# Mamba stack: half the square of the clipped exponential formed on ScalarE, softplus in four VectorE instructions per half, silu of z in the window that uses it

## The chip, the cores and the metric

The kernel runs on one core of a Trainium2 chip. The metric is the device time in microseconds (us) of one execution; the median of three runs of the kernel before is 5499.93 us (5496.72 to 5500.54).

## The reference

Four Mamba layers run over a batch of four sequences (64 conditioning tokens in front of 512 tokens, width 256, inner width 512, 16 states), and three transformer layers follow, which the change does not touch. One Mamba block, cut to what matters:

```python
xz = einsum('bsd,ed->bse', rmsnorm(h, norm_w), ip_w)
xi, z = split(xz, 2, axis=-1)
xi = silu(causal_conv(xi, cw) + cb)
dt, Bm, Cm = split(einsum('bse,fe->bsf', xi, xp_w), [DR_, DR_ + DS_], axis=-1)
dt = softplus(einsum('bsr,er->bse', dt, dtp_w) + dtp_b)
dA = exp(dt[..., None] * -exp(A_log))
dBu = dt[..., None] * Bm[:, :, None, :] * xi[..., None]
# scan over time: h = dA * h + dBu;  y = sum over states of h * C
y = (y + xi * Dp) * silu(z)
h = h + einsum('bse,de->bsd', y, op_w)
```

Softplus of v is taken as relu(v) + log(1 + e) with e = exp(-|v|). The kernel uses the logarithm of (1 + e) / (1 + EDGE) for large e and the series m - m*m/2 with m = min(e, EDGE), EDGE = 2^-11, for what is below.

## The kernel before, in words

The Mamba stack is 16 units of work, one per layer and batch entry, and the code walks them in "windows": window n does the scan of unit n, the preparation of unit n+1 and the end of unit n-1 together. Window -1 only prepares unit 0; it is the prologue. Channels lie on the 128 partitions; a unit has 4 chunks of 128 channels by T = 576 tokens, and a "half" is two chunks, 1152 columns. A window has 32 steps j: 16 states for either half.

In step j each engine has a fixed share of the scan, written out by hand:

- ScalarE (ACT), `decay(j)`, line 515: two exponentials of 128x575 make DA for step j. It is issued two steps ahead, and may be at most four steps ahead of the scan, since DA has four buffers. Decays 0 and 1 of a window wait for the semaphore s_dt, with which VectorE says that the step sizes DT of that unit are complete.
- VectorE (DVE), `drive(j)`, line 630, multiplies DTX by the row of B into PSUM (U); `recur(j)`, line 638, is the scan of 128x1152. The scan waits for its DA (semaphore s_da).
- GpSimd (POOL), line 571, multiplies the states by C; TensorE (PE), line 356, adds them up into Y.

Between these steps the preparation of the next unit is placed by tables. `PREP_AT` gives the steps of the TensorE products and of the ScalarE reads behind them: the mean square "ms" in step 0, the projections "xz" (0 to 3 for x, 4 to 7 for z), the convolution "cv", "xp", and "dt" in steps 24 to 27. In step 0 ScalarE also squares the stream for the norm (line 437), TensorE sums the squares (ms), and ScalarE takes the logarithm and exponential of the sum (lines 442 and 444); `norm()` on VectorE (line 598) uses that after step 3.

`prep_read("dt", i)` on ScalarE writes relu(v) to DT and |v| to E (a view of XPAD), and after every second chunk the exponential E (line 471) and the logarithm LG (line 472), and raises s_sp. `softplus(k, part_two)` on VectorE, lines 606 to 622, then finishes a half. `SOFTPLUS` places part one of the first half behind step 27, part two behind 28, and those of the second half behind 30 and 31. Part two of the second half raises s_dt.

`silu_z` on ScalarE, lines 504 to 507, loads the table with silu, applies it to all 2304 columns of z of unit n+1, and loads the table of exp and ln again. `SILU_Z` places it in step 30. `gate` on VectorE (line 645) multiplies Y by silu(z): the first half of a unit behind step 17 of its own window, the second half behind step 2 of the next one.

Of the kernel before, what the change touches and what calls it, by code (L numbers as in the profile page):

```python
# [6 lines left out]
ALU = mybir.AluOpType  # L7
# [3 lines left out]
P = 128  # L11
D = 256
KD = D // P
# [3 lines left out]
START = 1  # L17
# [13 lines left out]
PAD = DC - 1  # L31
EDGE = 2.0 ** -11
SHRINK = 1.0 / (1.0 + EDGE)
NBC = 2 * DS
NXP = NBC + DR

# [36 lines left out]
           16: ("xz", 4), 18: ("cv", 2), 20: ("cv", 3), 22: ("xp", 0), 23: ("xz", 5), 24: ("dt", 0), 25: ("dt", 1),  # L73
           26: ("dt", 2), 27: ("dt", 3), 28: ("xz", 6), 29: ("xz", 7)}
END_AT = {6: ("O", 0), 8: ("O", 1)}
SILU_X, SILU_Z = 21, 30

SOFTPLUS = {27: (0, False), 28: (0, True), 30: (KD, False), 31: (KD, True)}
NBB = 4
# [22 lines left out]
def mamba_stack(nc, hT, IDENT, wa, wb, x_t, ctx_t, pre_w, ones, fin_norm):  # L102
# [3 lines left out]
    with ctx:  # L106
# [15 lines left out]
        FIN = sb("FIN", [P, KD])  # L122
        EPSC = sb("EPSC", [P, 1])
        SHRC = sb("SHRC", [P, 1])
        HN = sb("HN", [P, KD, T])
        RSTD = sb("RSTD", [P, T])
        XPAD = sb("XPAD", [P, KI, PAD + T])
# [79 lines left out]
        with nc.Block() as block:  # L207
# [191 lines left out]
            def _(act):  # L399
# [12 lines left out]
                def body(n, scan, prep, end):  # L412
# [3 lines left out]
                    npar = nxt % 2  # L416
                    off = npar * (KI * T)
                    hb = (nxt % NB) * T
                    k0 = 8
                    step = [0]  # L420

                    def own(ins, wait=True):
# [16 lines left out]
                    def prep_read(kind, i):  # L439
                        full(kind, i)  # L440
                        if kind == "ms":
                            own(act.activation(half(RSTD[:, :]), pair, ACT.Ln, bias=EPSC[:, 0:1]))
                            act.sem_inc(s_free, 1)
                            act.activation(RSTD[:, :], RSTD[:, :], ACT.Exp, scale=-0.5).then_inc(s_rstd, 1)
                        if kind == "xz" and i < KI:
                            act.activation(half(XPAD[:, i, PAD:PAD + T]), pair, ACT.Copy).then_inc(s_xi, 1)
                            act.wait_ge(s_xi, START + nxt * KI + i + 1)
                            act.sem_inc(s_free, 1)
                        if kind == "xz" and i >= KI:
                            act.activation(half(ZS[:, bass.ds(off + (i - KI) * T, T)]), pair, ACT.Copy).then_inc(s_z, 1)  # L450
                            act.wait_ge(s_z, START + nxt * KI + i - KI + 1)
                            act.sem_inc(s_free, 1)
                        if kind == "cv":
                            act.activation(half(XS[:, bass.ds(off + i * T, T)]), pair, ACT.Identity,
                                           bias=WA[:, A_CB + i:A_CB + i + 1]).then_inc(s_conv, 1)
                            act.wait_ge(s_conv, START + nxt * KI + i + 1)
                            act.sem_inc(s_free, 1)  # L457
                        if kind == "xp":
                            if scan:
                                act.wait_ge(s_rows, 16 * nxt)  # L460
                            act.activation(half(BCF[:, :]), PAIR[0:NXP, :, 0:HT], ACT.Copy).then_inc(s_bcf, 1)
                            act.wait_ge(s_bcf, START + nxt + 1)
                            act.sem_inc(s_free, 1)
                        if kind == "dt":
                            bias = WA[:, A_DTB + i:A_DTB + i + 1]
                            act.activation(half(DT[:, bass.ds(off + i * T, T)]), pair, ACT.Relu, bias=bias)
                            own(act.activation(E[:, i, :].rearrange("p (a n) -> p a n", a=2), pair, ACT.Abs, bias=bias))
                            act.sem_inc(s_free, 1)
                            if i % 2:
                                two = slice(i - 1, i + 1)  # L470
                                own(act.activation(E[:, two, :], E[:, two, :], ACT.Exp, scale=-1.0))
                                act.activation(LG[:, two, :], E[:, two, :], ACT.Ln, bias=SHRC[:, 0:1],
                                               scale=SHRINK).then_inc(s_sp, 1)
                            if i == KI - 1:
                                own(act.activation(ALOG[:, :], WA[:, A_LOG:A_COLS], ACT.Exp))
                                act.activation(NEGA[:, bass.ds(npar * (KI * DS), KI * DS)], ALOG[:, :], ACT.Copy,
                                               scale=-1.0).then_inc(s_nega, 1)
# [25 lines left out]

                    def silu_z():
                        act.preload_act_table_set("silu_and_others")
                        act.activation(ZS[:, bass.ds(off, KI * T)], ZS[:, bass.ds(off, KI * T)], ACT.Silu).then_inc(s_zs, 1)
                        act.preload_act_table_set("natural_log_exp_and_others")

                    def decay(j):
# [15 lines left out]
                    for j in range(NJ):  # L525
                        if prep and j == 0:
                            squares()
                        if prep and j == SILU_X:
                            silu_x()
                        if prep and j == SILU_Z:  # L530
                            silu_z()
                        if scan and j + 2 < NJ:
                            decay(j + 2)
                        if prep and j in (2, 3) and nxt % NB == 0:
                            diagonals(j - 2)
                        for kind, i in slot_uses(j, prep, end):
                            if kind == "O":
                                stream(i)
                            else:
                                prep_read(kind, i)  # L540
                    assert not prep or step[0] == k0, step
                act.wait_ge(s_zero, START + 3)
                act.wait_ge(s_dvec, 16 * NL)
                act.wait_ge(s_const, 32)
                windows(body)
# [12 lines left out]
            def _(pool):  # L558
                pool.memset(EPSC[:, :], EPS).then_inc(s_zero, 1)
                pool.memset(SHRC[:, :], SHRINK).then_inc(s_zero, 1)  # L560
                pool.memset(DA[:, :, :], 0.0).then_inc(s_zero, 1)

                def body(n, scan, prep, end):
# [12 lines left out]
            def _(dve):  # L576
                def body(n, scan, prep, end):
# [4 lines left out]
                    hb = (nxt % NB) * T  # L582
                    eoff = par * (KI * T)
                    uses, base = window_uses(prep, end), before(n, N_PREP, N_END)
                    k_prep = 10
                    start = before(n, k_prep, 0)
                    step = [0]

# [17 lines left out]
                    def softplus(k, part_two):  # L606
# [2 lines left out]
                        o = off + k * T  # L609
                        dt = DT[:, bass.ds(o, KD * T)].rearrange("p (c t) -> p c t", c=KD)  # L610

                        e, ln, part = E[:, k:k + KD, :], LG[:, k:k + KD, :], E[:, k:k + KD, :]
                        if not part_two:
                            own(dve.tensor_scalar(part, e, EDGE, -0.5, ALU.min, ALU.mult))
                            own(dve.scalar_tensor_tensor(out=part, in0=part, scalar=1.0, in1=part, op0=ALU.add, op1=ALU.mult))
                        else:
                            own(dve.scalar_tensor_tensor(out=dt, in0=part, scalar=-2.0, in1=dt, op0=ALU.mult, op1=ALU.add))
                            own(dve.scalar_tensor_tensor(out=dt, in0=ln, scalar=0.0, in1=dt, op0=ALU.max, op1=ALU.add))
                            own(dve.tensor_tensor(DTX[:, bass.ds(o, KD * T)], DT[:, bass.ds(o, KD * T)],
                                                  XS[:, bass.ds(o, KD * T)], ALU.mult))  # L620
                            if k:
# [1148 lines left out]
```

## Time and profile before

| | |
|---|---|
| median of three runs | 5499.93 us |
| the profiled execution's own time | 5501.36 us |
| its span, first to last instruction | 5499.6 us |
| PE busy | 4949.9 us (90%) |
| DVE busy | 3920.6 us (71%) |
| POOL busy | 2606.0 us (47%) |
| ACT busy | 2303.9 us (42%) |
| Mamba stack, of the span | 0 to about 2465 us |

Busy shares are means over two very different parts. In the Mamba part (the first 18 of the 40 slices of the page) VectorE is busy nearly all of the time; in the transformer part TensorE is. Idle time in front of an instruction is printed in square brackets in the timeline, with the engine or queue that ended it.

### The profile page before, as it was taken

To read this page: it belongs to the slowest core of one execution; us is meant where nothing else is said; L and a number is where in the kernel's file an instruction comes from. 1 tells how busy PE (TensorE), PEld (TensorE's weight loads), DVE (VectorE), ACT (ScalarE), POOL (GpSimd) and SP (SyncE) were. 2 spreads that over 40 slices of the span, in tenths; PEclk is the share of its full clock that TensorE was granted. 3 is DMA by queue.
4 is the path that set the end of the run, shared out by engine and by line. 5 is a ranking of instruction groups with operands and counts; after the bars stand their busy time and mean duration, and the time that the engine had idled before them with its cause. 6 is when DMAs were issued, how large, how long until landed. Compare 5 with 4: busy or idle time off the path is not lost.

```text
span 5499.6 us, 53836 instructions
## 1 busy us (share of the span) xinstructions
PE 4949.9 (90%) x18976; PEld 2623.3 (48%) x18976; DVE 3920.6 (71%) x3886; ACT 2303.9 (42%) x4022; POOL 2606.0 (47%) x1334
## 2 busy tenths in 40 slices
PE   5888898888888888877999889999999999999999
PEld 3455555555555555433444444444444444444444
DVE  2999999999999999974767552666656246665641
ACT  3555654455555555523444333333333233333321
POOL 1555555555555555554777212666610036665000
PEclk8999999999999999987999999999999999999999
DMA  2434444444444444321000010000000000001000
GB/s 78 142 132 148 145 147 147 142 144 144 144 144 140 140 144 144 134 107 36 1 1 21 19 39 1 1 1 1 10 38 31 8 1 1 1 1 47 0 1 16
DMA packets 94440, 376.70 MB, mean 68 GB/s; under 512 B 13024, under 2 KB 14432, under 8 KB 91232
## 3 DMA queue, kind: packets, MB, share of 16 engines
q1 hardware_dynamic: 94176, 373.26, 19.4%
q8 instruction: 157, 2.57, 0.2%
q14 instruction: 107, 0.88, 0.1%
HBM read 369.94 MB, written 3.28 MB: 68 GB/s over the span
## 4 chain that ended last, share of the span: by engine, by line
PE 43%; DVE 6%; POOL 3%; issue 1%; ACT 1%; DMA 0%; SPq 0%; DVEq 0%; ACTq 0%
PE PS L1061 6%; PE PS L1085 6%; PE PS L1071 5%; PE PS L1246 5%; PE PS L1040 5%; PE PS L1257 3%; POOL PA L1004 3%; PE PS L1049 3%; PE PS L1095 3%; PE PS L1206 2%; PE PS L1170 1%; PE PS L1158 1%; DVE PA L1582 1%; DVE CST L1580 1%; DVE NMX L1494 1%
## 5 line engine op out<-in xcount | busy, mean ns | idle before, releaser
L571 POOL TENSOR_TENSOR UH<-UH,BC 128x1152 f32<-128x1152 f32 x512 | 1343.7, 2624 | 1094.2 <-DVE U L630 1094.2
L1004 POOL TENSOR_SCALAR PA<-PA,INV 128x512 f32<-128x512 f32 x768 | 1188.1, 1563 | 647.8 <-DVE INV L1500 645.4
L356 PE MATMUL Y<-UH,ident_sb 128*128 128x512 f32 (+1 forms) x3072 | 1171.1, 526 | 226.4 <-POOL UH L571 171.8
L638 DVE TENSOR_TENSOR_SCAN UH<-DA,U 128x1152 f32<-128x1152 f32 x512 | 1307.2, 2553 | 21.2 <-ACT DA L515 3.8
L356 PEld LDWEIGHTS Y<-UH,ident_sb 128*128 128x128 f32 x3072 | 591.3, 203 | 844.9 <-issue 569.9
L1317 ACT ACTIVATE PA<-PS,NMX 128x512 f32<-128x512 f32 x768 | 521.0, 683 | 1028.9 <-DVE NMX L1494 1002.8
L515 ACT ACTIVATE DA<-DT,NEGA 128x575 f32<-128x575 f32 x1024 | 718.8, 763 | 333.5 <-DVEq L622 237.5
L630 DVE TENSOR_TENSOR U<-DTX,BC 128x1152 f32<-128x1152 f32 x512 | 701.1, 1369 | 49.5 <-DVEq L622 4.2
L1494 DVE TENSOR_REDUCE NMX<-PS 128x2 f32<-128x1024 f32 x384 | 467.8, 1219 | 242.6 <-PE PS L1061 242.3
L1509 DVE COPY VP<-PS 128x512 f32<-128x512 f32 x768 | 491.9, 681 | 32.2 <-PE PS L1071 31.7
L1071 PEld LDWEIGHTS PS<-ident_sb,PA 128*128 128x128 f32 x3072 | 330.1, 142 | 327.4 <-issue 195.3
L1071 PE MATMUL PS<-ident_sb,PA 128*128 128x128 f32 x3072 | 437.3, 282 | 21.5 <-POOL PA L1004 20.6
L1061 PE MATMUL PS<-QK 64*128 64x512 f32 (+1 forms) x1536 | 435.9, 645 | 4.7 <-issue 2.5
L1085 PE MATMUL PS<-VP 128*64 128x256 f32 (+1 forms) x3072 | 375.0, 386 | 0.1
L992 POOL TENSOR_TENSOR LSQ<-stream 128x512 f32<-128x512 f32 x21 | 26.6, 1266 | 694.8 <-DVE stream L1599 437.7
L1040 PE MATMUL PS<-HN,W 128*128 128x512 f32 x640 | 309.8, 606 | 5.1 <-DVEq L1489 2.9
L312 PE MATMUL PAIR<-HN,WA 128*128 128x288 f32 x1024 | 278.3, 416 | 14.6 <-DVE HN L598 6.4
L1246 PE MATMUL PS<-HN,VP 128*128 128x512 f32 x640 | 288.6, 592 | 2.7 <-issue 2.7
L1486 DVE TENSOR_SCALAR QK<-PS,VEC 128x512 f32<-128x512 f32 x80 | 64.8, 810 | 303.7 <-PE PS L1040 303.7
L1085 PEld LDWEIGHTS PS<-VP 128*64 128x64 f32 (+1 forms) x3072 | 191.3, 128 | 168.7 <-issue 46.2
L312 PE MATMUL PAIR<-XPAD,DG 128*128 128x288 f32 x1024 | 259.8, 406 | 3.3 <-ACTq L457 1.8
L1634 DVE SCALAR_TENSOR_TENSOR QK<-PS,VEC,QK 128x512 f32<-128x512 f32 x64 | 48.1, 751 | 244.5 <-ACT QK L1413 244.5
(133 smaller groups left out, 5443.1 us busy)
## 6 DMA issues: line engine op xcount, KB each, us to landing
BC<-bc_rows SPq DMA_DIRECT2D x512, 576.0 KB, 3.7
WA<-mamba_a SPq DMA_DIRECT2D x16, 1421.0 KB, 7.4
W<-pair_w SPq DMA_DIRECT2D x6, 3072.0 KB, 10.4
WB<-mamba_b SPq DMA_DIRECT2D x16, 514.0 KB, 5.0
VP<-ff_w SPq DMA_DIRECT2D x2, 3072.0 KB
WO<-out_w SPq DMA_DIRECT2D x4, 1024.0 KB
stream<-x_t SPq DMA_DIRECT2D x2, 1024.0 KB, 6.9
VP<-ff_w SPq DMA_DIRECT2D x2, 1024.0 KB
```

Source lines behind the costliest of these rows:

```text
L312: mm = pe.matmul(PAIR[0:out_rows, a, 0:HT], lhs, rhs(a), start=start, stop=stop)
L356: mm = pe.matmul(Y[:, a:b], IDENT[:, :], UH[:, SLOT[j], a:b], start=(s == 0), stop=(s == DS - 1), skip_group_check=True)
L515: ins = act.activation(DA[:, j % NDA, c * T + 1:(c + 1) * T], DT[:, bass.ds(par * (KI * T) + cc * T + 1, T - 1)], ACT.Exp, scale=NEGA[:, b ...
L571: pool.tensor_tensor(h, h, BC[:, j % NBB, 1, :].unsqueeze(1).broadcast_to([P, HK, T]), ALU.mult).then_inc(s_hc, 1)
L630: dve.tensor_tensor(u, x, BC[:, j % NBB, 0, :].unsqueeze(1).broadcast_to([P, HK, T]), ALU.mult).then_inc(s_u, 1)
L638: dve.tensor_tensor_scan(UH[:, SLOT[j], :], DA[:, j % NDA, :], U[:, 0:HC], 0.0, ALU.mult, ALU.add).then_inc(s_scan, 1)
L1004: pool.tensor_scalar(PR[:, n % 3, j, :], PR[:, n % 3, j, :], INV[:, n % 4, j:j + 1], None, ALU.mult).then_inc(s_ps, 1)
L1040: mm = pe.matmul(PS[:, B_J, :], w_tile(l, "qk".index(kind), t, k), HN[:, k, b * S0:(b + 1) * S0], start=(k == 0), stop=(k == KD - 1))
L1061: mm = pe.matmul(PS[:, B_S + 2 * (n % 2) + j, :], Q[r:r + HW[l], tt % 2, qt * P:(qt + 1) * P], K[r:r + HW[l], tt % 2, :], start=True, stop ...
L1071: mm = pe.transpose(PS[:, B_T + j, kt * P:(kt + 1) * P], PR[:, n % 3, j, kt * P:(kt + 1) * P], IDENT[:, :])
L1085: mm = pe.matmul(PS[r:r + HW[l], B_V, half * 256:(half + 1) * 256], VT[:, tt // QT % 2, kt, c:c + HW[l]], PT[:, hh % 2, kt, j, :], start=( ...
L1246: mm = pe.matmul(PS[:, 2 * (f % 2) + g, :], w1[:, k, c:c + P], HN[:, k, b * S0:(b + 1) * S0], start=(k == 0), stop=(k == KD - 1))
```

## The change

The silu of z goes from step 30 of the window that prepares the unit to step 1 of the window that scans it. ScalarE forms half the square of m, by a relu and a square of 128x1152 per half, and puts it into DTX, which is free until the product with x is written there. VectorE then adds the logarithm and m to DT in part one, and subtracts the half square and multiplies by x in part two: four instructions per half where there were five. Two memsets of GpSimd in the prologue fill the constants EDGC.

```diff
-SILU_X, SILU_Z = 21, 30
+SILU_X, SILU_Z = 21, 1
...
                             if i % 2:
                                 two = slice(i - 1, i + 1)
                                 own(act.activation(E[:, two, :], E[:, two, :], ACT.Exp, scale=-1.0))
-                                act.activation(LG[:, two, :], E[:, two, :], ACT.Ln, bias=SHRC[:, 0:1],
-                                               scale=SHRINK).then_inc(s_sp, 1)
+                                act.activation(LG[:, two, :], E[:, two, :], ACT.Ln, bias=SHRC[:, 0:1], scale=SHRINK)
+                                sq = DTX[:, bass.ds(off + (i - 1) * T, KD * T)].rearrange("p (c t) -> p c t", c=KD)
+                                own(act.activation(sq, E[:, two, :], ACT.Relu, bias=EDGC[:, 0:1], scale=-1.0))
+                                act.activation(sq, sq, ACT.Square, bias=EDGC[:, 1:2], scale=-HALF_ROOT).then_inc(s_sp, 1)
...
                     def silu_z():
                         act.preload_act_table_set("silu_and_others")
-                        act.activation(ZS[:, bass.ds(off, KI * T)], ZS[:, bass.ds(off, KI * T)], ACT.Silu).then_inc(s_zs, 1)
+                        act.activation(ZS[:, bass.ds(par * (KI * T), KI * T)], ZS[:, bass.ds(par * (KI * T), KI * T)],
+                                       ACT.Silu).then_inc(s_zs, 1)
                         act.preload_act_table_set("natural_log_exp_and_others")
...
-                        if prep and j == SILU_Z:
+                        if scan and j == SILU_Z:
                             silu_z()
...
-                        e, ln, part = E[:, k:k + KD, :], LG[:, k:k + KD, :], E[:, k:k + KD, :]
+                        e, ln = E[:, k:k + KD, :], LG[:, k:k + KD, :]
                         if not part_two:
-                            own(dve.tensor_scalar(part, e, EDGE, -0.5, ALU.min, ALU.mult))
-                            own(dve.scalar_tensor_tensor(out=part, in0=part, scalar=1.0, in1=part, op0=ALU.add, op1=ALU.mult))
+                            own(dve.scalar_tensor_tensor(out=dt, in0=ln, scalar=0.0, in1=dt, op0=ALU.max, op1=ALU.add))
+                            own(dve.scalar_tensor_tensor(out=dt, in0=e, scalar=EDGE, in1=dt, op0=ALU.min, op1=ALU.add))
                         else:
-                            own(dve.scalar_tensor_tensor(out=dt, in0=part, scalar=-2.0, in1=dt, op0=ALU.mult, op1=ALU.add))
-                            own(dve.scalar_tensor_tensor(out=dt, in0=ln, scalar=0.0, in1=dt, op0=ALU.max, op1=ALU.add))
+                            own(dve.tensor_tensor(DT[:, bass.ds(o, KD * T)], DT[:, bass.ds(o, KD * T)],
+                                                  DTX[:, bass.ds(o, KD * T)], ALU.subtract))
                             own(dve.tensor_tensor(DTX[:, bass.ds(o, KD * T)], DT[:, bass.ds(o, KD * T)],
                                                   XS[:, bass.ds(o, KD * T)], ALU.mult))
```

The first place is ScalarE at the turn from window 0 to window 1 (every later turn is alike). The rows of before begin at the last read of z. DA rows are decays, two to a step; the four together are those of steps 0 and 1, the next two are step 2, the last ones step 3 and on.

```order
L450 ACTIVATE ZS<-PAIR 128x576
L505 ACT_TABLE_LOAD
L506 ACTIVATE ZS<-ZS 128x2304
L507 ACT_TABLE_LOAD
L515 ACTIVATE DA<-DT,NEGA 128x575 x4
L437 ACTIVATE HN<-stream 128x1152
L515 ACTIVATE DA<-DT,NEGA 128x575 x2
L442 ACTIVATE RSTD<-PAIR,EPSC 128x576
L444 ACTIVATE RSTD<-RSTD 128x576
```

The same place in the changed kernel, whose line numbers are a few higher:

```order
L452 ACTIVATE ZS<-PAIR 128x576
L520 ACTIVATE DA<-DT,NEGA 128x575 x4
L439 ACTIVATE HN<-stream 128x1152
L520 ACTIVATE DA<-DT,NEGA 128x575 x2
L444 ACTIVATE RSTD<-PAIR,EPSC 128x576
L446 ACTIVATE RSTD<-RSTD 128x576
L509 ACT_TABLE_LOAD
L510 ACTIVATE ZS<-ZS 128x2304
L512 ACT_TABLE_LOAD
```

The block of two table loads and the silu stood ahead of the decays of step 0; now it stands behind the norm's exponential and ahead of the decays of step 3.

The second place is VectorE behind steps 27 and 28 of a window. L638 is the scan, L630 the drive of the next step. Before:

```order
L638 SCALAR_TENSOR_TENSOR UH<-DA,U 128x1152
L614 TENSOR_SCALAR XPAD<-XPAD 128x2x576
L615 SCALAR_TENSOR_TENSOR XPAD<-XPAD 128x2x576
L630 TENSOR_TENSOR U<-DTX,BC 128x1152
L638 SCALAR_TENSOR_TENSOR UH<-DA,U 128x1152
L617 SCALAR_TENSOR_TENSOR DT<-XPAD,DT 128x1152
L618 SCALAR_TENSOR_TENSOR DT<-LG,DT 128x1152
L619 TENSOR_TENSOR DTX<-DT,XS 128x1152
L630 TENSOR_TENSOR U<-DTX,BC 128x1152
```

And now, with L645 as the scan and L637 as the drive:

```order
L645 SCALAR_TENSOR_TENSOR UH<-DA,U 128x1152
L621 SCALAR_TENSOR_TENSOR DT<-LG,DT 128x1152
L622 SCALAR_TENSOR_TENSOR DT<-XPAD,DT 128x1152
L637 TENSOR_TENSOR U<-DTX,BC 128x1152
L645 SCALAR_TENSOR_TENSOR UH<-DA,U 128x1152
L624 TENSOR_TENSOR DT<-DT,DTX 128x1152
L626 TENSOR_TENSOR DTX<-DT,XS 128x1152
L637 TENSOR_TENSOR U<-DTX,BC 128x1152
```

Behind the first scan a tensor_scalar is replaced by a scalar_tensor_tensor; behind the second one of three instructions is gone, and the first of the two left is a tensor_tensor.

The third place is ScalarE at the fourth read of dt, in step 27. Before:

```order
L467 ACTIVATE XPAD<-PAIR,WA 128x576
L471 ACTIVATE XPAD<-XPAD 128x2x576
L472 ACTIVATE LG<-XPAD,SHRC 128x1152
L475 ACTIVATE ALOG<-WA 128x64
L476 ACTIVATE NEGA<-ALOG 128x64
L515 ACTIVATE DA<-DT,NEGA 128x575 x2
```

And now:

```order
L469 ACTIVATE XPAD<-PAIR,WA 128x576
L473 ACTIVATE XPAD<-XPAD 128x2x576
L474 ACTIVATE LG<-XPAD,SHRC 128x1152
L476 ACTIVATE DTX<-XPAD,EDGC 128x1152
L477 ACTIVATE DTX<-DTX,EDGC 128x1152
L479 ACTIVATE ALOG<-WA 128x64
L480 ACTIVATE NEGA<-ALOG 128x64
L520 ACTIVATE DA<-DT,NEGA 128x575 x2
```

Two instructions of 128x1152 stand between the logarithm and what followed it; the same two stand behind the logarithm of the first half.

## Rows read from the trace of the kernel before

**Rows 1.** Page, part 2: VectorE's busy tenths in 40 slices

```profile
DVE  2999999999999999974767552666656246665641
```

**Rows 2.** Stages: stretch, length, busy us of each engine, clock, DMA

```profile
111.00:2312.00 2201.00, 1907.77 (x6194) 1134.67 (x6194) 2127.61 (x1185) 1174.21 (x1591) 1257.45 (x479) 0.93 0.41 143
```

**Rows 3.** VectorE's groups by line and shape, 0 to 2300 us

```profile
L638 DVE TENSOR_TENSOR_SCAN UH<-DA,U 128x1152 f32<-128x1152 f32 x479 | 1222.9, 2553 | 20.0 <-ACT DA L515 3.8
L630 DVE TENSOR_TENSOR U<-DTX,BC 128x1152 f32<-128x1152 f32 x479 | 656.0, 1370 | 46.2 <-DVEq L622 4.0 <-DVE UH L638 1.9
L617 DVE SCALAR_TENSOR_TENSOR DT<-XPAD,DT 128x1152 f32<-128x1152 f32 x31 | 45.5, 1468 | 0.1
L615 DVE SCALAR_TENSOR_TENSOR XPAD<-XPAD 128x1152 f32<-128x1152 f32 x31 | 42.1, 1359 | 1.1
L614 DVE TENSOR_SCALAR XPAD<-XPAD 128x1152 f32<-128x1152 f32 x31 | 27.0, 871 | 60.4 <-ACT LG L472 60.4
```

**Rows 4.** VectorE's timeline behind steps 27 and 28 of window 3

```profile
671.27 0.88 DVE L614 TENSOR_SCALAR XPAD<-XPAD 128x1152 f32<-128x1152 f32 x1
...
673.57 1.37 DVE L630 TENSOR_TENSOR U<-DTX,BC 128x1152 f32<-128x1152 f32 x1
...
677.44 1.49 DVE L617 SCALAR_TENSOR_TENSOR DT<-XPAD,DT 128x1152 f32<-128x1152 f32 x1
...
681.75 1.37 DVE L630 TENSOR_TENSOR U<-DTX,BC 128x1152 f32<-128x1152 f32 x1
```

**Rows 5.** ScalarE's timeline at the turn from window 3 to 4

```profile
674.59 1.42 ACT L515 ACTIVATE DA<-DT,NEGA 128x575 f32<-128x575 f32 x2
...
680.55 1.28 ACT L505 ACT_TABLE_LOAD   x1
...
683.98 1.28 ACT L507 ACT_TABLE_LOAD   x1
700.20 2.77 ACT L515 ACTIVATE DA<-DT,NEGA 128x575 f32<-128x575 f32 x4 [14.93 <-DVEq L622]
702.87 1.15 ACT L437 ACTIVATE HN<-stream 128x1152 f32<-128x1152 f32 x1
...
709.46 2.75 ACT L515 ACTIVATE DA<-DT,NEGA 128x575 f32<-128x575 f32 x4
```

**Rows 6.** VectorE's scans: step 30 of window 3, steps 0 and 3 of window 4

```profile
687.21 2.55 DVE L638 TENSOR_TENSOR_SCAN UH<-DA,U 128x1152 f32<-128x1152 f32 x1
...
701.75 2.55 DVE L638 TENSOR_TENSOR_SCAN UH<-DA,U 128x1152 f32<-128x1152 f32 x1
...
714.98 2.55 DVE L638 TENSOR_TENSOR_SCAN UH<-DA,U 128x1152 f32<-128x1152 f32 x1
```

**Rows 7.** TensorE's sum of squares in window 4, from its timeline

```profile
704.16 3.81 PE L312 MATMUL PAIR<-HN,ONES 128*128 128x288 f32 x8 [4.80 <-ACT HN L437]
```

**Rows 8.** ScalarE's decays of steps 0 and 3, windows 3 and 14

```profile
553.81 2.77 ACT L515 ACTIVATE DA<-DT,NEGA 128x575 f32<-128x575 f32 x4 [16.10 <-DVEq L622]
...
562.88 2.76 ACT L515 ACTIVATE DA<-DT,NEGA 128x575 f32<-128x575 f32 x4
...
2165.92 2.77 ACT L515 ACTIVATE DA<-DT,NEGA 128x575 f32<-128x575 f32 x4 [16.22 <-DVEq L622]
...
2175.55 2.75 ACT L515 ACTIVATE DA<-DT,NEGA 128x575 f32<-128x575 f32 x4
```

**Rows 9.** Prologue and window 0, timelines of ScalarE and VectorE

```profile
104.79 0.76 DVE L614 TENSOR_SCALAR XPAD<-XPAD 128x1152 f32<-128x1152 f32 x1 [1.36 <-ACT LG L472]
116.47 2.55 DVE L638 TENSOR_TENSOR_SCAN UH<-DA,U 128x1152 f32<-128x1152 f32 x1 [3.76 <-ACT DA L515]
...
128.64 2.55 DVE L638 TENSOR_TENSOR_SCAN UH<-DA,U 128x1152 f32<-128x1152 f32 x1
...
103.43 1.26 ACT L472 ACTIVATE LG<-XPAD,SHRC 128x1152 f32<-128x1152 f32 x1
...
114.93 2.77 ACT L515 ACTIVATE DA<-DT,NEGA 128x575 f32<-128x575 f32 x4
...
124.56 2.09 ACT L515 ACTIVATE DA<-DT,NEGA 128x575 f32<-128x575 f32 x3
```

More of the change, by code:

```diff
@@ L33 @@
 SHRINK = 1.0 / (1.0 + EDGE)
+HALF_ROOT = 0.5 ** 0.5
 NBC = 2 * DS
@@ L124, in mamba_stack @@
         SHRC = sb("SHRC", [P, 1])
+        EDGC = sb("EDGC", [P, 2])
         HN = sb("HN", [P, KD, T])
@@ L418, in body @@
                     hb = (nxt % NB) * T
-                    k0 = 8
+                    k0 = 10
                     step = [0]
@@ L541, in body @@
                     assert not prep or step[0] == k0, step
-                act.wait_ge(s_zero, START + 3)
+                act.wait_ge(s_zero, START + 5)
                 act.wait_ge(s_dvec, 16 * NL)
@@ L560, in _ @@
                 pool.memset(SHRC[:, :], SHRINK).then_inc(s_zero, 1)
+                pool.memset(EDGC[:, 0:1], EDGE).then_inc(s_zero, 1)
+                pool.memset(EDGC[:, 1:2], EDGE * HALF_ROOT).then_inc(s_zero, 1)
                 pool.memset(DA[:, :, :], 0.0).then_inc(s_zero, 1)
@@ L584, in body @@
                     uses, base = window_uses(prep, end), before(n, N_PREP, N_END)
-                    k_prep = 10
+                    k_prep = 8
                     start = before(n, k_prep, 0)
```

## Prediction

> **What bounds the kernel now.** I read the page's slices first. VectorE stands at 9 tenths in slices 2 to 17, the Mamba part [rows 1]. Over windows 0 to 14 the stage table gives VectorE 2127.61 of 2201.00 us, or 97%, and ScalarE 1174.21, or 53% [rows 2]. The groups by line then say what VectorE's idle time is: ahead of 479 drives 46.2 us and ahead of 479 scans 20.0 us, about 0.1 us each, the handover from one to the next; the only wait for a decay is 3.8 us in all [rows 3], and it lies in the prologue [rows 9]. So no other engine holds VectorE up once the scans run. An instruction taken from it there shortens the kernel by its own length, and each wait that it gets lengthens it. What comes behind the Mamba part starts when that part ends and is not touched.
>
> ScalarE looks free, but its free time is not spread evenly. At each turn between windows it waits for s_dt, 14.93 us here, 16.10 and 16.22 at two others [rows 5, 8]. The silu block sits in front of that wait and costs nothing there. Behind the wait, ScalarE has no lead at all: it has made no DA yet, and four steps' worth must be ready by step 3. That is where the block goes.
>
> **Term 1: VectorE's instructions in softplus.** Before, part one takes 673.57 - 671.27 = 2.30 us from its first start to the drive, and part two 681.75 - 677.44 = 4.31 us [rows 4]. Together 6.61 us per half. Of the new four instructions, three kinds are known: a scalar_tensor_tensor of this size takes 1.36 us when it follows with a wait (line 615) [rows 3], and 1.47 us when it starts right behind a scan (line 617) [rows 3]; the step from one to the next is 0.03 us more. Part one becomes 1.50 + 1.39 = 2.89 us. Part two becomes a tensor_tensor behind a scan and another one. The drive, also a tensor_tensor of 128x1152, takes 1.37 us (line 630) [rows 3], so 1.39 for the second. For the first, whose output is in SBUF and which starts behind a scan, I have no row. Its bounds are 1.36, as alone, and 1.49, as the longest here of the kind behind a scan (line 617) [rows 4]; I take 1.47, since it too has two inputs and follows a scan without a wait. Part two is then 1.50 + 1.39 = 2.89 us. New sum 5.78 us, a gain of 0.83 us per half, with bounds of 0.81 and 0.94. Windows 0 to 14 hold 30 halves: **-24.9 us**, between -24.3 and -28.2.
>
> The gain is small because the removed group is the cheap one: a tensor_scalar of 0.87 us (line 614) [rows 3]. The removed scalar_tensor_tensor is made up for by the new subtraction.
>
> **Term 2: the silu block behind the norm.** In window 4 ScalarE gets s_dt at 700.20. It makes the decays of 0 and 1, the squares, the decay of 2; then it waits for TensorE's sum of squares, which starts at 704.16, right after the squares, and takes 3.81 us [rows 5, 7]. The decay of step 3 starts at 709.46, 9.26 us after s_dt. Now the block comes in between. It lasts from 680.55 to 683.98 + 1.28 = 685.26, 4.71 us [rows 5]. From the start of a decay pair to the scan that waits for it are 116.47 - 114.93 = 1.54 us, by the one place where a scan waits for one [rows 9]. So the scan of step 3 can start at 9.26 + 4.71 + 1.54 = 15.51 us after s_dt. It starts at 714.98 - 700.20 = 14.78 us now [rows 5, 6], and everything ahead of it on VectorE (three steps and the gate of the second half) stays. That makes a wait of 0.73 us in this window; generally it is (distance from s_dt to the decay of 3) - 8.53. The distance is 9.07 in window 3, the shortest, and 9.63 in window 14 [rows 8]; over the 14 windows 1 to 14 its mean is 9.50, as most are at 9.63. Mean wait 0.97, times 14: **+13.6 us**, with 7.6 if all were like window 3 and 15.4 if all were like window 14.
>
> Window 0 has no gate, so its scan 3 comes earlier, at 128.64. The decay of 3 would start at 124.56 + 4.71, its scan at 130.81: **+2.2 us** [rows 9]. Window 15 has no norm to wait for: its decay of 3 stands behind three decays and the block, some 4.1 + 4.7 = 8.8 us after s_dt, and costs nothing.
>
> Queued behind the block are only decays. From step 3 on ScalarE needs 1.4 us per step, VectorE 1.37 + 2.55 and more, so the lead is back by step 5 or 6. The diagonals of windows 3, 7 and 11 (20 copies in steps 2 and 3, some 5.8 us) come after the decays of 4 and 5 and still leave step 6 its DA.
>
> **Term 3: two ScalarE operations per half.** The nearest rows are the square of 128x1152 at 1.15 us (line 437) [rows 5] and the logarithm at 1.26 (line 472) [rows 9]; I take 1.2 each. In the windows they delay the decays of 29 to 31 and the reads of z by 2.4 and then 4.8 us. Decay 30 starts at 674.59; at 679.4 it would still be ready at 680.9, with its scan at 687.21 [rows 5, 6]. 6 us of slack are left. TensorE's last dt and z products wait for those reads and delay the sums of steps 25 to 27, but a scan needs a sum only four steps later. The s_dt wait loses no time, as the 14.93 us stay: the block's 4.7 us leave it, the added 4.8 enter. Cost: nothing. If that cover were gone, it would be up to 4.8 us per window.
>
> The prologue has no cover. The second s_sp, 104.79 now, comes 4 x 1.2 us later, at 109.6, since dt is read one chunk after the other; four instructions of 1.39 bring s_dt to 115.1, the first decay to 115.2 and the first scan to 116.8, against 116.47 [rows 9]. There the block had stood between, and its going saves what the new operations add: **+0.3 us**.
>
> **Sum.** -24.9 + 13.6 + 2.2 + 0.3 = -8.8 us. Against the profiled execution's own 5501.36 that is 5492.6. That execution lies 1.4 us above the median of the runs, so 5491 us on the scale of the median.
>
> **A rule weighed.** The rows show the block as 4.71 us, of which the two loads are 1.28 each and nothing is left between [rows 5]. The Trainium skill (ScalarE: Activation LUTs, section "What ACT_TABLE_LOAD costs") gives the same 1.28 us but adds a drain of about 1.38 for every switch, 2.66 in all. By that rule the block behind the decays would take about 7.4 us, an estimate, and the sum would come out near +32. The trace speaks against it.
>
> **Rivals.**
>
> - *The wait is shorter (14%).* The sum of squares takes 3.81 us at a clock that has dropped while TensorE was idle; window 3 has the shortest distance. If the shorter gap at the turn keeps the higher clock, all windows are like window 3 or better: -24.9 + 7.6 + 1.6 + 0.3 = -15.4, 5484.5. Against it: TensorE is still idle 4 us there.
> - *No wait at all (6%).* ScalarE's place proves free, as its 53% busy suggests: -24.9 + 0.3 = -24.6, 5475. Against it are the times of rows 5 and 6.
> - *Slower: the block holds ScalarE longer when it stands behind exponentials (4%).* Before, it always stood behind a copy or an identity. If each of its two loads first waited for the exponential in front to drain, for as long again as a load lasts (1.28 us), the block would be 7.3 us, and scan 3 would wait 2.6 us more in 15 windows, +39: +30 us, 5530. It decides from a block of 5.3 us on, where no gain is left, and shows as slower from 6.0. The rule weighed above lies on this side.
> - *Slower: ScalarE late at the end of the windows (3%).* If the two operations cost over 3 us each, or TensorE's sums came late, scan 30 would wait. Its slack is 6 us; from there each us of lateness is 15 us, so 1.5 us beyond it end at +14, 5514.
> - *The two terms cancel (7%).* The tensor_tensor or the scalar_tensor_tensor behind the scan costs 0.2 us more than I took: -3, 5497.
>
> **How the numbers follow.** 0.2%, or 11 us, is about what a measurement of this kernel can tell from no change. The forecast itself has 66%, with 5485 to 5495 by its bounds (-28.2 + 13 + 2.5 at one end, -24.3 + 15.4 + 2.5 + 1 at the other). It crosses the 11 us for some 14 of these 66. Faster: 14 + 14 + 6 = 34%. Slower: 4 + 3 = 7%. Same: 52 + 7 = 59%. The range leaves out "no wait at all", the slower rivals and their like: 5479 to 5500.
>
> **What would show it.** VectorE's idle time ahead of the scans, put down to DA, should rise from 3.8 us to some 16 to 18, in 15 pieces, one per window at step 3: 0.5 to 1.2 us each and 2.2 in window 0. The 3.76 us in the prologue should be gone. The first instructions of parts one and two should read 1.47 us, the second ones 1.36. ScalarE's wait for s_dt should remain near 15 us. Most dangerous to the number is the distance from s_dt to the decay of step 3, since every 0.1 us of it is 1.5 us of the result.

## The result, and the profile after

The changed kernel takes 5485.98 us (median of 20 runs, 5471.53 to 5492.46), the kernel before 5496.33 us (median of 20, 5481.84 to 5504.88). The ratio is 0.9984 with a 95% interval of [0.9977, 0.9991]: between 5 and 13 us less, 8.8 by the ratio and 10.4 by the two medians. 5485.98 is inside the stated range of 5479 to 5500, 5 us below the 5491 of the forecast, and the change is within the 0.2% which was the likeliest case. Of those 5 us, 3.6 come from the starting point: the forecast took 5499.93 for the kernel before, from three runs. The profiled execution has a span of 5483.3 us against 5499.6.

The runs of one kernel lie up to 23 us apart, so much of what follows is read from the timelines of single executions, by two numbers: when the first scan starts, and the time from the first to the last scan of the Mamba part, called the stack. There is one profile of each kernel. What lies behind the last scan, untouched by any kernel here, took 3052.5 to 3058.0 us in the eleven profiles. The first scan starts at 117.28 (before 116.47), the last one at 2430.49 (before 2441.61): 2313.21 us between them against 2325.14.

The groups of VectorE, 0 to 2300 us; columns as in [rows 3]:

```profile
L645 DVE TENSOR_TENSOR_SCAN UH<-DA,U 128x1152 f32<-128x1152 f32 x480 | 1225.5, 2553 | 30.2 <-issue 6.3 <-DVE U L637 5.3 <-ACT DA L520 2.3
...
L624 DVE TENSOR_TENSOR DT<-DT,DTX 128x1152 f32<-128x1152 f32 x32 | 47.0, 1468 | 0.1
L621 DVE SCALAR_TENSOR_TENSOR DT<-LG,DT 128x1152 f32<-128x1152 f32 x32 | 46.8, 1463 | 67.0 <-ACT DTX L477 67.0
L622 DVE SCALAR_TENSOR_TENSOR DT<-XPAD,DT 128x1152 f32<-128x1152 f32 x32 | 43.5, 1358 | 1.1
L626 DVE TENSOR_TENSOR DTX<-DT,XS 128x1152 f32<-128x1152 f32 x32 | 43.5, 1358 | 1.1
```

The four softplus instructions cost what was taken for them: 1.46 and 1.47 us behind a scan, 1.36 else. The new price is in the first row: the scans' idle time rose from 20.0 us to 30.2, while a wait of 3.8 us at the first scan went. The added ScalarE work, by its groups over the same stretch:

```profile
L477 ACT ACTIVATE DTX<-DTX,EDGC 128x1152 f32<-128x1152 f32 x32 | 40.2, 1255 | 1.0
L476 ACT ACTIVATE DTX<-XPAD,EDGC 128x1152 f32<-128x1152 f32 x32 | 39.7, 1242 | 0.0
```

And the turn from window 3 to 4 on ScalarE, the place of [rows 5]:

```profile
698.41 2.77 ACT L520 ACTIVATE DA<-DT,NEGA 128x575 f32<-128x575 f32 x4 [13.24 <-DVEq L629]
...
708.15 1.28 ACT L509 ACT_TABLE_LOAD   x1
709.45 2.12 ACT L510 ACTIVATE ZS<-ZS 128x2304 f32<-128x2304 f32 x1
711.59 1.28 ACT L512 ACT_TABLE_LOAD   x1
712.88 3.43 ACT L520 ACTIVATE DA<-DT,NEGA 128x575 f32<-128x575 f32 x5
```

The block (load, silu, load) takes 712.88 - 708.15 = 4.73 us up to the next decay, and the decay of step 3 starts 14.47 us after s_dt. VectorE at step 3 of windows 0, 3 and 4, the places of [rows 6, 9]:

```profile
131.76 2.55 DVE L645 TENSOR_TENSOR_SCAN UH<-DA,U 128x1152 f32<-128x1152 f32 x1 [2.33 <-ACT DA L520]
...
567.27 2.55 DVE L645 TENSOR_TENSOR_SCAN UH<-DA,U 128x1152 f32<-128x1152 f32 x1
...
714.41 2.55 DVE L645 TENSOR_TENSOR_SCAN UH<-DA,U 128x1152 f32<-128x1152 f32 x1 [1.25 <-issue]
```

Window 4 waits 1.25 us, window 3 does not wait, window 0 waits 2.33. Over all windows these waits sum to 13.9 us; 12 of the windows 1 to 14 have one of 0.4 to 1.3 us, windows 3 and 6 none. The reader should not trust the name "issue" here: the scan starts 714.41 - 712.88 = 1.53 us after the decay pair does, the 1.54 us of [rows 9], so it is the decay that ends the wait. What makes windows differ is TensorE's sum of squares, here in windows 3 and 4:

```profile
556.46 2.18 PE L314 MATMUL PAIR<-HN,ONES 128*128 128x288 f32 x8 [2.41 <-ACT HN L439]
...
702.38 4.18 PE L314 MATMUL PAIR<-HN,ONES 128*128 128x288 f32 x8 [2.41 <-ACT HN L439]
```

The same eight products, after the same idle time, take 2.18 us in the one and 4.18 in the other. The stage table of these two stretches (length, busy us of PE, PEld, DVE, ACT, POOL, granted clock, DMA) has the reason in its third last column:

```profile
556.00:560.00 4.00, 3.54 (x12) 2.39 (x13) 3.86 (x3) 2.85 (x5) 2.58 (x2) 1.00 0.58 148
702.00:707.00 5.00, 4.62 (x9) 3.19 (x10) 4.76 (x4) 1.97 (x4) 3.31 (x2) 0.50 0.64 204
```

The granted clock is 1.00 in window 3 and 0.50 in window 4, the levels of 2.4 and 1.2 GHz. The other windows from 1 to 14 bear it out: wherever the sum took 3.35 to 4.18 us, the scan of step 3 waited for that time less 2.92 us (window 10, with a wait of 0.36 us already at its first scan, for 3.25 less), and in windows 3 and 6, where the sum took 2.18, it did not wait.

### The profile page after: what moved, and what is told of

It is laid out like the page before. It is cut to its first block, busy times and chain, and to the rows that moved or that the text cites. A ratio compares the mean times of both kernels' runs of the same rounds, so it can differ in the third digit from the quotient of the medians.

```text
span 5483.3 us, 53870 instructions
## 1 busy us (share of the span) xinstructions
PE 4951.0 (90%) x18976; PEld 2624.3 (48%) x18976; DVE 3894.5 (71%) x3854; ACT 2380.7 (43%) x4086; POOL 2606.4 (48%) x1336
## 4 chain that ended last, share of the span: by engine, by line
PE 43%; DVE 6%; POOL 3%; issue 1%; ACT 1%; DMA 0%; SPq 0%; DVEq 0%; ACTq 0%
PE PS L1068 6%; PE PS L1092 6%; PE PS L1078 5%; PE PS L1253 5%; PE PS L1047 5%; PE PS L1264 3%; POOL PA L1011 3%; PE PS L1056 3%; PE PS L1102 3%; PE PS L1213 2%; PE PS L1177 1%; DVE PA L1589 1%; PE PS L1165 1%; DVE CST L1587 1%; DVE NMX L1501 1%
## 5 line engine op out<-in xcount | busy, mean ns | idle before, releaser
L645 DVE TENSOR_TENSOR_SCAN UH<-DA,U 128x1152 f32<-128x1152 f32 x512 | 1307.2, 2553 | 31.3 <-issue 6.3
L637 DVE TENSOR_TENSOR U<-DTX,BC 128x1152 f32<-128x1152 f32 x512 | 701.1, 1369 | 49.1 <-DVEq L629 3.9
L314 PE MATMUL PAIR<-HN,WA 128*128 128x288 f32 x1024 | 283.2, 421 | 33.7 <-ACTq L454 16.6
L314 PEld LDWEIGHTS PAIR<-HN,WA 128*128 128x128 f32 x1024 | 192.1, 198 | 86.0 <-ACTq L454 20.3
## 6 DMA issues: line engine op xcount, KB each, us to landing
W<-pair_w SPq DMA_DIRECT2D x6, 3072.0 KB, 10.7
```

The lines of the kernel that those rows point to most:

```text
L314: mm = pe.matmul(PAIR[0:out_rows, a, 0:HT], lhs, rhs(a), start=start, stop=stop)
L637: dve.tensor_tensor(u, x, BC[:, j % NBB, 0, :].unsqueeze(1).broadcast_to([P, HK, T]), ALU.mult).then_inc(s_u, 1)
L645: dve.tensor_tensor_scan(UH[:, SLOT[j], :], DA[:, j % NDA, :], U[:, 0:HC], 0.0, ALU.mult, ALU.add).then_inc(s_scan, 1)
```

## The experiments

Each ratio is against runs of the kernel before that were measured together with that kernel's. First scan and stack are in us, from the one profile of each kernel, and are compared with the one profile of the kernel before.

| kernel | ratio, 95% interval | first scan | stack |
|---|---|---|---|
| before | | 116.47 | 2325.14 |
| changed | 0.9984 [0.9977, 0.9991] | 117.28 | 2313.21 |
| softplus only | 0.9969 [0.9959, 0.9979] | 119.19 | 2301.77 |
| silu only | 1.0018 [1.0009, 1.0027] | 113.14 | 2337.47 |
| silu in step 9 | 0.9994 [0.9986, 1.0003] | 117.64 | 2319.45 |
| added TensorE products | 0.9983 [0.9975, 0.9992] | 116.22 | 2314.56 |
| silu in step 3 | 0.9967 [0.9953, 0.9980] | 117.39 | 2306.13 |
| same, relu three times | 0.9993 [0.9985, 1.0002] | 122.78 | 2317.32 |
| silu in step 0 | 0.9995 [0.9986, 1.0003] | 117.20 | 2315.10 |
| silu in step 30, unit 0 in step 3 | 0.9960 [0.9947, 0.9972] | 116.73 | 2301.73 |
| silu in step 3, gate behind 18 | 0.9966 [0.9953, 0.9978] | 117.61 | 2311.72 |

**The softplus part alone.** The changed kernel, with the silu back in step 30. The cut (...) leaves out that `silu_z` takes `off` again, the offset of the unit being prepared.

```diff
-SILU_X, SILU_Z = 21, 1
+SILU_X, SILU_Z = 21, 30
...
-                        if scan and j == SILU_Z:
+                        if prep and j == SILU_Z:
```

> The changed kernel with the silu of z back in step 30 of the window that prepares the unit, so only the softplus part of the change is left. My theory (two terms that add): VectorE's gain of 0.83 us per half stays, -25 us over 30 halves; no scan of step 3 waits for a decay; in the prologue the block stands in front of the first decay again, behind the two added ScalarE operations, so the first scan comes some 5.5 us later than before (about 122). Sum near -19.5 us against the kernel before. Rival (the waits at step 3 are not the block's doing, they come from the added ScalarE work or from the shorter turn): the waits stay, 10 us or more in all, and the time is that of the changed kernel, about -9. Rival (the softplus part gives less than the rows said): -12 or less with no waits at step 3.

The stack is 23.4 us shorter, with no wait at step 3. Scan to scan, in the mean over windows 1 to 14 against the kernel before, steps 27 and 30 are 0.59 and 0.61 us longer and steps 28 and 31 are 1.39 and 1.40 us shorter, all others within 0.12: 0.80 us per half where I had 0.83. The ratio says 17 us less than before, between 12 and 23, where I had 19.5. The first scan behind its wait:

```profile
119.19 2.55 DVE L644 TENSOR_TENSOR_SCAN UH<-DA,U 128x1152 f32<-128x1152 f32 x1 [4.68 <-ACT DA L519]
```

So the rival that the waits come from the added ScalarE work falls. The first scan came 2.7 us later than before, not 5.5.

**The move of the silu alone**, the kernel before with `SILU_Z = 1`, `if scan` and the offset of unit n.

> The kernel before with only the move of the silu of z to step 1 of the window that scans the unit; softplus in five VectorE instructions. My theory: a wait at the scan of step 3 in most windows, 0 to 1.3 us each and 2.2 in window 0, 12 to 16 us in all; the prologue's 3.8 us wait for the first decay goes. Sum +8 to +12 us against the kernel before, the wait in each window following the distance from s_dt to the decay of step 3. Rival (the block is hidden, the changed kernel's waits belong to the added operations): -3.5 us, the prologue's part alone, and no waits at step 3.

```profile
L639 DVE TENSOR_TENSOR_SCAN UH<-DA,U 128x1152 f32<-128x1152 f32 x477 | 1217.8, 2553 | 33.0 <-issue 11.1 <-DVE U L631 3.8 <-ACT DA L516 2.3
```

Slower by 5 to 15 us: its stack is 12.3 longer and its first scan 3.3 earlier. Waits at step 3 sum to 17.3 us, in all of windows 0 to 14. Not all of it lands in the stack: the distance from scan 17 to 18, where the gate stands, is 3.1 us shorter in sum than before. Together the two halves give -23.4 + 12.3 = -11.1 of stack, against -11.9 for the changed kernel, so they add to within 1 us.

**The silu in step 9**, `SILU_X, SILU_Z = 21, 9`.

> The changed kernel with the silu of z in step 9 of its window instead of step 1, when ScalarE has a lead of several decays. My theory: the block is hidden, no scan waits for a decay, and the whole softplus gain is left: -24 to -26 us against the kernel before, first scan at about 117. Rival (the block costs ScalarE's lead wherever it stands, as a wait for a decay or a late read of a TensorE product): waits of about 1 us per window move to steps 9 to 13, and the time is within 3 us of the changed kernel's, about -9.

My theory was wrong. The rival was right about the waits, which moved to step 11; the time was not within 3 us of the changed kernel's but some 5 us above it, by the ratios (0.9994 against 0.9984) and by the stack (6.2 us longer). ScalarE and VectorE in window 4:

```profile
739.93 0.65 ACT L485 ACTIVATE stream<-PAIR 128x576 f32<-128x576 f32 x1 [5.19 <-PE PAIR L314]
740.75 1.28 ACT L509 ACT_TABLE_LOAD   x1 [0.17 <-ACT stream L485]
...
745.49 2.77 ACT L520 ACTIVATE DA<-DT,NEGA 128x575 f32<-128x575 f32 x4
```

```profile
747.01 2.55 DVE L645 TENSOR_TENSOR_SCAN UH<-DA,U 128x1152 f32<-128x1152 f32 x1 [1.34 <-ACT DA L520]
```

ScalarE had stood still for 5.19 us, for TensorE's second output product, and the block came right behind that. A ScalarE that idles is not one with a lead: its queue is in order, and the decays behind the read were held as well. Scan 11 waits 1.3 to 1.6 us in 12 windows, 16.6 in all. In the run with the softplus part alone, where no block stands there, the data of decay 11 are ready 3.5 us before the scan in the median of windows 1 to 14; the block of 4.7 us is 1.2 longer than that.

**The silu in step 3**, `SILU_X, SILU_Z = 21, 3`, chosen by the lead of each step: the time from the moment a decay's data are ready to the scan that reads them.

> The changed kernel with the silu of z in step 3. The silu in step 9 stood right behind ScalarE's read of the second output product in step 8, for which it had waited, so its lead was small, and scan 11 waited 1.34 us in 12 of 15 windows. From the trace of the run with the silu in step 30 I worked out, for each step, how long before its scan a decay's data is ready: 0 in step 0, 3.6 us in step 3, at least 7.3 us in steps 4 to 6, 2.2 in step 11, 2.9 in 9 and 15, 2.1 in 23. My theory (a place is free if the next decays all have more than the block's 4.7 us): behind step 3 the decays of 5 and on are touched, with 7.3 us and more, so no scan waits; -24 us in the windows and +0.8 in the prologue, -23 against the kernel before. Rival (the block costs about 1 us wherever it stands, or pushes TensorE's products): a wait of 0.5 us or more per window in steps 4 to 11, and -15 or less.

No scan waits for a decay in any window, so the rule on the lead held. The stack is 19.0 us shorter, not 24, and the ratio says 18 less, not 23: the distance from scan 17 to 18 is 5.0 us longer in sum over the windows than before. There the gate waits for TensorE's sums, as in window 3:

```profile
626.00 1.36 DVE L652 TENSOR_TENSOR ZS<-Y,ZS 128x1152 f32<-128x1152 f32 x1 [1.68 <-PE Y L358]
```

**The silu in step 0**, `SILU_X, SILU_Z = 21, 0`, so that it overlaps the sum of squares.

> The changed kernel with the silu of z in step 0, behind the squares and ahead of the decay of step 2, so that it overlaps TensorE's sum of squares instead of following it. Theory: the decay of step 2 starts some 8.5 us after s_dt and scan 2, now 9.7 us after it, can start at 10.0: a wait of 0.3 us in each of 15 windows, always the same because no TensorE clock enters it, 4.8 us in all; -18.5 against the kernel before. Rival (what costs is that the block stands near the start of the window at all): waits of 1 us or more as in the changed kernel, -9.

```profile
702.08 1.28 ACT L509 ACT_TABLE_LOAD   x1
703.37 2.12 ACT L510 ACTIVATE ZS<-ZS 128x2304 f32<-128x2304 f32 x1
705.51 1.28 ACT L512 ACT_TABLE_LOAD   x1
706.81 1.44 ACT L520 ACTIVATE DA<-DT,NEGA 128x575 f32<-128x575 f32 x2
708.15 0.72 ACT L444 ACTIVATE RSTD<-PAIR,EPSC 128x576 f32<-128x576 f32 x1
```

```profile
708.34 2.55 DVE L645 TENSOR_TENSOR_SCAN UH<-DA,U 128x1152 f32<-128x1152 f32 x1 [0.47 <-ACT DA L520]
```

Behind the block the sum is there at once. Scan 2 waits 0.46 or 0.47 us in twelve windows, whether the sum took 3.4 or 4.2 us, and 0.81 in window 2: 6.9 us in all where I had 4.8. The rest of the gap to my -18.5 is once more the step from scan 17 to 18, 7.6 us longer in sum than before. By the last scan (2432.30) the kernel gains 9.3 us; by the ratio it is within noise of no change.

**TensorE kept busy at the turn.** The products write into PAIR, which the sum of squares overwrites; they add work and leave the result as it is.

```diff
+WARM_A, WARM_B = 10, 6
...
                         if kind == "ms":
+                            if scan:
+                                for r in range(WARM_B):
+                                    pe.matmul(PAIR[:, 0, 0:P], ONES[:, :], IDENT[:, :], start=True, stop=True)
                             pe.wait_ge(s_sq, START + nxt + 1)
...
                     for j in range(NJ):
+                        if scan and prep and j == 0:
+                            pe.wait_ge(s_free, START + base)
+                            for r in range(WARM_A):
+                                pe.matmul(PAIR[:, 0, 0:P], ONES[:, :], IDENT[:, :], start=True, stop=True)
                         if end and j < 2:
                             add_up(NJ - 2 + j, n - 1)
```

> The changed kernel with 16 more TensorE products of 128x128 per window into the unused PAIR buffer, overwritten right after: 10 in front of the sum of step 30 of the unit before and 6 in front of the sum of squares, where TensorE stood idle 4.6 and 2.4 us. Theory (the spread of the waits at step 3, 0 to 1.3 us, is TensorE's clock in the sum of squares): the granted clock at the turn stays at its higher level, the sum of squares takes 2.2 us in all windows as it did in windows 3 and 6 of the changed kernel, the distance from s_dt to the decay of step 3 is 12.5 us, and the waits of windows 1 to 14 vanish: 11 us less than the changed kernel, -20 against the one before. Rival (the spread comes from elsewhere, such as the stream's tail or ScalarE's own queue): distances stay between 13.6 and 14.5, and the time is the changed kernel's, or up to 5 us more for the added products.

Half of it came true. In eight windows (0, 1, 2, 5, 6, 9, 13 and 14) the sum of squares took 2.21 us. In window 0 the wait at step 3 fell from 2.33 to 0.27, in the other seven there is none. In the remaining seven windows the sum took 3.8 to 4.2 us, and there the wait stayed. Windows 6 and 7:

```profile
991.49 2.21 PE L315 MATMUL PAIR<-HN,ONES 128*128 128x288 f32 x8 [2.97 <-ACT HN L447]
...
1137.86 4.21 PE L315 MATMUL PAIR<-HN,ONES 128*128 128x288 f32 x8 [2.98 <-ACT HN L447]
```

```profile
1002.39 2.55 DVE L653 TENSOR_TENSOR_SCAN UH<-DA,U 128x1152 f32<-128x1152 f32 x1
...
1149.92 2.55 DVE L653 TENSOR_TENSOR_SCAN UH<-DA,U 128x1152 f32<-128x1152 f32 x1 [1.19 <-issue]
```

The waits at step 3 fell from 13.9 to 7.1 us, but the stack did not get shorter: the distance from scan 17 to 18 grew by 7.4 us in sum against the changed kernel. By the ratio (0.9983) the kernel is where the changed kernel is, and not 11 us below it. So the level of the clock in the sum of squares decides the wait at step 3. The added products raise it only in some windows, and there the clock was at its lower level later: in each of windows 1, 2, 5, 6, 9, 13 and 14 from 10 or 11 us to 17 or 18 us after the window's first scan, and the distance from scan 17 to 18 was 1.1 to 1.7 us above its shortest, 5.11.

**More ScalarE work ahead of s_sp.** The silu in step 3, and the relu over the same data three times (`own(act.activation(sq, E[:, two, :], ACT.Relu, ...))` twice more; `k0`, ScalarE's count of operations that it waits for itself, goes from 10 to 14).

> As the kernel with the silu in step 3, and with the added relu of either half made three times over the same data, 4 x 1.2 = 4.8 us more ScalarE work per window ahead of s_sp. My theory (the two added operations are hidden at the end of the windows, with some 4.5 us of slack left at scan 30): no waits in windows 0 to 14 or only fractions of a us at scan 30; the prologue alone takes the 4.8 us. -18 against the kernel before. Rival (ScalarE's work ahead of s_sp is on VectorE's path): up to 4.8 us in each of 15 windows, 0 to +50 against the kernel before.

```profile
398.07 2.55 DVE L647 TENSOR_TENSOR_SCAN UH<-DA,U 128x1152 f32<-128x1152 f32 x1 [0.68 <-ACT DA L522]
...
405.87 2.55 DVE L647 TENSOR_TENSOR_SCAN UH<-DA,U 128x1152 f32<-128x1152 f32 x1 [1.21 <-PE Y L358]
```

The prologue took 5.4 us of it (first scan 122.78 against 117.39). Ten windows have a wait of 0.45 to 0.74 us at scan 30, 6.2 in all, and four have one for TensorE at scan 31, 4.5 in all. So the two operations of the change are hidden, but 4.8 us more use up their cover. The forecast of -18 was missed: the ratio says 4 us less than before, and the stack is 11.2 us longer than with the silu in step 3 alone, of which these waits are 10.7. By the time only (0.9993) one could not have told where it went.

**Silu in step 30 again, save for unit 0.** The best of both: the changed softplus, the block where ScalarE waits for s_dt anyway, and not in the prologue.

```diff
-SILU_X, SILU_Z = 21, 1
+SILU_X, SILU_Z = 21, 30
...
-                        if scan and j == SILU_Z:
-                            silu_z()
+                        if prep and not end and scan and j == 3:
+                            silu_z(par * (KI * T))
+                        if scan and prep and j == SILU_Z:
+                            silu_z(off)
```

> The changed softplus with the silu of z in step 30 of the preparing window, as in the kernel before, save that the prologue leaves it out and window 0 makes it up for unit 0 in step 3. The run with the silu in step 30 alone had no wait at step 3 and its stack was 23.4 us shorter from first to last scan, but its first scan came at 119.2 behind a wait of 4.7 us for the first decay. My theory: this one has the first scan at 117.3 and the 23.4 us, so the last scan near 2419 and -22 to -23 against the kernel before; the fastest of all. Rival (the window's end was free only since the phase of TensorE's clock happened to fit): gate waits at step 17 as with the silu in step 3, and -18.

First and last scan:

```profile
116.73 2.55 DVE L646 TENSOR_TENSOR_SCAN UH<-DA,U 128x1152 f32<-128x1152 f32 x1 [0.46 <-ACT DA L519]
...
2418.46 2.55 DVE L646 TENSOR_TENSOR_SCAN UH<-DA,U 128x1152 f32<-128x1152 f32 x1
```

5472.26 us (median of 5 runs) against 5491.34, a ratio of 0.9960 [0.9947, 0.9972]: some 22 us less than before, 23.2 by the last scan. Its ratio and its last scan are the lowest of this study, and its interval lies below that of the changed kernel; it overlaps those of the softplus part alone and of the silu in step 3, with the gate behind 17 or behind 18. The rival's waits at the gate did not come: the distances from scan 17 to 18 sum to 87.4 us, against 87.2 with the softplus part alone. These two kernels differ for unit 0 only, and their stacks (2301.73 and 2301.77) show how well two single profiles can agree.

**The gate behind step 18.** With the silu in step 3, and `if scan and j == 18:` for the first gate.

> The changed kernel with the silu in step 3 and the gate of the first half behind step 18 instead of 17. In the run with the silu in step 3 the distance between scans 17 and 18 summed over the windows was 5 us longer than before (91.8 against 86.7), with the gate waiting for TensorE's sums up to 1.6 us. My theory (TensorE is late there, by its backlog at the lower clock, and the gate is what waits): a step later the sums are done, the distance returns to that without a wait, and the stack is 6 to 8 us shorter than with the gate at 17: -24 against the kernel before. Rival (TensorE's next sums wait for the gate, so the lateness only moves): waits for Y appear at the scans of steps 20 to 23, and the time stays at -18 or is worse.

The rival was right in kind, but the wait came for a decay, not for Y. The wait at the gate went, but TensorE's sums of the second half wait for the gate, and the last convolution behind them comes later to ScalarE, which then does the silu of x and only then the decay of 23:

```profile
1373.50 0.74 ACT L456 ACTIVATE XS<-PAIR,WA 128x576 f32<-128x576 f32 x1 [12.35 <-PE PAIR L314]
...
1379.07 2.77 ACT L520 ACTIVATE DA<-DT,NEGA 128x575 f32<-128x575 f32 x4
```

```profile
1380.60 2.55 DVE L645 TENSOR_TENSOR_SCAN UH<-DA,U 128x1152 f32<-128x1152 f32 x1 [2.76 <-ACT DA L520]
```

Scan 23 waits in eight windows, 13.9 us in all; the stack is 5.6 us longer than with the gate behind 17. The ratios of the runs (0.9966 and 0.9967) cannot tell the two apart.

## Why the prediction was right

Its two terms that pull against each other are both there, each shown alone.

*Term 1, softplus.* Predicted -24.9 us, measured -23.4 of stack in the run with it alone; 0.80 us per half lies just below the stated bounds of 0.81 to 0.94. The tensor_tensor behind a scan, for which there was no row, took 1.468 us, the value chosen from the scalar_tensor_tensor in the same place. Its lower bound, 1.36, is wrong there.

*Term 2, the silu block.* Predicted waits of 13.6 us in windows 1 to 14 and 2.2 in window 0; measured 11.6 and 2.3. The mechanism is the one worked out: a block of 4.7 us, the decay of step 3 behind it, 1.53 us to the scan. What was mis-sized is the distance from s_dt to that decay, the number named as the most dangerous. I took its lower end from window 3, 9.07 us, as the best case; without the block of 4.72 us it was 7.75 in windows 3 and 6 of the changed kernel, where the sum of squares ran at the higher clock throughout (2.18 us), and 8.9 to 9.8 elsewhere. The rival "the wait is shorter" thus came true in two windows of fourteen, and for its reason, the clock. That all windows get the higher clock stayed out of reach even with added products.

*Term 3, two ScalarE operations.* 1.24 and 1.26 us against the 1.2 taken, hidden in the windows: the wait for s_dt is still 14.3 us in the mean. The "6 us of slack" at scan 30 was too much for most windows: measured like that it is 4.5 to 7.2 us in the changed kernel, and 4.5 in window 3, where I had read it off. Of the 11.1 us there before, the four operations took 4.9, a wait for TensorE's fourth dt product, which came later too, took 0.9, and VectorE's own gain of 0.8 brought the scan nearer; I had counted only the first. That fits the waits of 0.5 to 0.7 us with 4.8 us more. The prologue lost 0.8 us, predicted 0.3.

*The sum.* -8.8 predicted, -8.8 by the ratio, -10.4 by the medians and -11.1 by the last scan. With the profiles' terms it is -24.0 from 30 halves of 0.80 us, 13.9 of waits less some 1.1 us because step 3 behind a wait is 0.07 shorter, and 0.8 in the prologue: -10.4. The agreement to the decimal is luck: the interval spans 8 us, and term 1 gave 1.5 us less than forecast while term 2 cost 1.9 less. One slip of the forecast had no effect: its bound of 5485 does not follow from its terms, as -28.2 + 13 + 2.5 gives 5487.

*The other rivals.* "No wait at all" and "the terms cancel" are out by the rows of step 3 and of the softplus group. "Table loads that drain first" is out: the 16 blocks, now behind exponentials, took 4.72 us each, as the blocks behind copies did. The Trainium skill (ScalarE: Activation LUTs, "What ACT_TABLE_LOAD costs") puts 2.66 us on a switch; here the trace shows 1.28 and no more.

*Not foreseen.* The distance from scan 17 to 18, with the gate and its wait for TensorE's sums, differs between kernels by up to 11 us in sum (83.6 in the run with the silu alone, 86.5 in the changed kernel, 94.5 with the relu made three times), although nothing was changed there. In many windows it is 5.11 us, in most others up to 0.6 longer, in some 0.9 to 1.8. In the profiles the long ones go with TensorE's clock. The stage table of the changed kernel for 11 to 17.5 us behind the first scan of windows 3 and 4 (columns as above):

```profile
565.00:571.50 6.50, 5.49 (x8) 2.61 (x9) 6.46 (x7) 6.50 (x16) 2.63 (x1) 0.50 0.32 129
711.00:717.50 6.50, 5.57 (x14) 2.83 (x15) 5.25 (x4) 6.47 (x9) 2.63 (x1) 0.74 0.34 113
```

In window 3 the clock is at 1.2 GHz all through, and its distance from scan 17 to 18 is 6.67 us; in window 4 only for about half of the time, and there it is 5.11. In the ten profiles with the gate in its old place, windows 1 to 14 hold 30 such stretches, at the lower level from 10 to 12 us after the first scan until 17 to 18.5; all 30 have a distance 0.9 to 1.8 us above 5.11. Of the 110 windows without one, 106 are at most 0.6 us above it; the four others are windows 7 and 11 of the kernel with the silu in step 3 and of the one with three relus, and in windows 3, 7 and 11 ScalarE also makes the diagonals. No run set the clock in that place alone, so this is an association and not a cause shown.

## What to carry to other kernels

Where one engine is the bound and another looks half idle, ask for its lead and not for its share: at each place in its queue, how long before its use is the next result ready? Here work moved there was free where it was shorter than the lead of every result behind it (step 3), and cost about the rest where it was not (steps 1 and 9); a place behind a wait (for the bound engine at a window's start, or for a product) had the least lead, however idle the engine was around it. And split a change that has two parts: here one part gave 23 us and the other took 12 back, and undoing the second, save for unit 0, made a faster kernel than the change as a whole.

## What the runs showed of the hardware that was not expected

The sum of squares, eight products of 128x288, took 2.18 us in two windows of the changed kernel and 3.35 to 4.18 in the thirteen others. The granted clock there was 1.00 in window 3 and 0.50 in window 4, with the same idle time of 2.41 us ahead of both, and a wait of 1.3 us on VectorE comes and goes with it. Sixteen added products per turn brought the higher level to eight windows of fifteen, with no gain in the time (0.9983 against 0.9984). Over all ten profiles with the gate behind step 17, in each of the fourteen windows from 1 to 14 with a sum of 2.2 us the clock was at its lower level 10 to 18 us behind the first scan instead, and the gate came 1.1 to 1.8 us later than at its best.
